# A spectral layer: TensorE's eight turns over the filters written out, and VectorE's matrix mixing put behind the third part of a unit

## The chip, the cores and the metric

The kernel runs on one core of one Trainium2 chip. The metric is the device time of one execution in microseconds (us). The kernel before takes 7840.03 us, the median of three runs from 7836.26 to 7846.94.

## The reference, cut to what matters

The program is a network of four layers over an image of 4 x 48 x 48 positions with 128 channels. The change touches only the last stage of layer 3, the spectral layer. It convolves every channel of the normalized stream with 16 causal filters, once as they are and once with the sign of every second position turned, and mixes the channels of each result with a 128x128 matrix:

```python
def _stu_conv(phi, u, n):
    sgn3 = where(arange(sl) % 2 == 0, 1.0, -1.0)[None, :, None]
    Vf, Uf_p, Uf_m = rfft(phi), rfft(u), rfft(u * sgn3)
    U_plus  = irfft(Vf[None, :, :, None] * Uf_p[:, :, None, :])[:, :sl]
    U_minus = irfft(Vf[None, :, :, None] * Uf_m[:, :, None, :])[:, :sl] * sgn
    return U_plus, U_minus

out = einsum('btkd,k,kde->bte', U_plus, sigma ** 0.25, Mpp) \
    + einsum('btkd,k,kde->bte', U_minus, sigma ** 0.25, Mpm)
# ... plus three shifted copies of u, each times a matrix; done for the whole
# sequence and its first half, quarter and eighth, each with its own matrices,
# and added with four weights; then t = t + result
```

Since the sum and the difference of U_plus and U_minus are convolutions with the even and the odd taps alone, the kernel mixes the two matrices of a filter into their sum (z = 0) and their difference (z = 1), and it adds the matrices of the four sequence lengths up, weighted, so that each stretch of the sequence meets one matrix.

## The kernel before, in words

`layer3_spectral` loops over the four images with `nc.Fori(0, NB)` (line 2301). Each image has a short block that orders and turns the input (L2303 to L2361), and then the block that matters here (from L2363). There each of the 16 filters gives four **units** (u % 4 = 0 to 3): the even or odd taps with the even or odd positions. One turn over a **pair** of filters is eight units, and an image has eight pairs. `r` (0 or 1) is the filter's place in the pair and the buffer it uses.

The work of a unit, engine by engine:

- TensorE (L2396 on) forms the convolution in three parts, by the sum-and-difference trick that saves products. `shared` (L2432), `shared_pairs` (L2442), `first` (L2422), `second` (L2432, L2442) and `third` (L2422, L2432) fill the PSUM banks OWN, PAIR and LOW for unit u + 1 while unit u is being mixed. The last `pairs` of unit u (L2442) comes at the head of its turn, and `mix` (L2457) multiplies each of the three finished parts with the filter's mixing matrices, in fp16 high and low pieces. Every unit is 108 matmuls.
- ScalarE (L2594 on) copies PSUM to SBUF (`keep`, `pair_1`), and writes the fp16 high piece of each finished part (`high`, L2607) and of the mixing matrices (L2611). It takes its instructions strictly in that order: `high` of the third part stands between `keep` of the next unit and the copy `pair_1` (L2619) of the next unit.
- VectorE (L2518 on) adds and subtracts to finish the parts: L2557 and L2558 the first, L2561 to L2564 the second, L2567 to L2579 the third. Between these it mixes the matrices of the next filter, `mix_step`: step 0 is two 128x512 operations (sum and difference, L2526 and L2527), each of steps 1 to 4 two 128x128 ones (L2537, L2539).
- GpSimd (L2636 on) subtracts the high piece from the value and so makes the low piece (`low`, L2641, 128x384; of the matrices L2645, 128x512).
- SyncE's DMA queue loads the next filter's taps (F, FS) and matrices (mab).

All engines run this as code with waits on semaphores, in the order in which the code stands. On TensorE and ScalarE the turns over pairs are a `Fori` loop of seven turns with the eighth written out behind it (the eighth prepares no next unit); on VectorE, GpSimd and the DMA queue they are a `Fori` loop of eight. In a filter the mixing steps stand so: unit 0 has steps 0 and 1, unit 1 steps 2 and 3, unit 2 step 4, unit 3 none; of each two the first stands between L2572 and L2576, that is inside the third part, and the second behind L2579.

What TensorE waits for in a unit: the copy `pair_1` before `pairs`; the high and low pieces before each `mix`; the combination L2569, which frees bank PAIR, before `shared_pairs`; L2572 before `first`.

Of the kernel before, what the change touches and what calls it, by code (L numbers as in the profile page):

```python
# [2074 lines left out]
KF, KU = 16, 3  # L2075
# [8 lines left out]
def layer3_spectral(nc, w, f_scr, f_sum, out):  # L2084
# [12 lines left out]
    with ExitStack() as ctx:  # L2097
# [203 lines left out]
        with nc.Fori(0, NB) as b:  # L2301
# [61 lines left out]
            with nc.Block() as block:  # L2363
# [31 lines left out]
                def _(pe):  # L2395
# [66 lines left out]
                    def shared(u):  # L2462
                        own(u, OWN, 2, 2 * HB + u % 2 * LB, True).then_inc(s_cv, 1)
# [24 lines left out]
                    def filters_pair(i, last):  # L2488
                        unit = (b * KF + i * 2) * NU
                        for u in range(2 * NU):  # L2490
                            r = u // NU
                            done = (unit + u) * 12 + 24
                            copied = (unit + u) * 4
                            v = (u + 1) % (2 * NU)
                            more = not (last and v == 0)
                            pe.wait_ge(s_ea, copied + 4)
                            pairs(u, FS[:, :, :, :, 1], 0, True).then_inc(s_cv, 1)
                            mix(i, u, 0)
                            if more:
                                if v % NU == 0:  # L2500
                                    pe.wait_ge(s_fl[v // NU], (b * (KF // 2) + i + (1 if v else 2)) * 64)
                                pe.wait_ge(s_ed, done + 3)
                                shared(v)
                                pe.wait_ge(s_ed, done + 7)
                                shared_pairs(v)
                            mix(i, u, 1)
                            if more:
                                pe.wait_ge(s_ed, done + 9)
                                first(v)
                                second(v, copied + 4)  # L2510
                                third(v, copied + 4)
                            mix(i, u, 2)

                    with pe.Fori(0, KF // 2 - 1) as i:
                        filters_pair(i, False)
                    filters_pair(KF // 2 - 1, True)

                @block.vector  # L2518
                def _(dve):
                    def mix_step(kk, i, r, step, total):  # L2520

                        if step == 0:
                            dve.wait_ge(s_ml[r], use(i, r) * 32 + 32)

                            dve.wait_ge(s_kd[r], b * (KF // 2) + i)
                            dve.tensor_tensor(Wm[:, r, 0], mab[:, r, 0], mab[:, r, 1], ALU.add).then_inc(s_ad[r], 1)  # L2526
                            dve.tensor_tensor(Wm[:, r, 1], mab[:, r, 0], mab[:, r, 1], ALU.subtract).then_inc(s_ad[r], 1)  # L2527
                            return
                        m = step - 1
                        if m == 0:  # L2530
                            dve.wait_ge(s_ad[r], use(i, r) * 2 + 2)
                        else:
                            dve.wait_ge(s_mm, total + 2 * m)
                        for z in range(2):
                            own, weight = Wm[:, r, z, m], mweight[:, ds(kk, 1), z, m:m + 1]
                            if m == 0:
                                ins = dve.tensor_scalar(own, own, weight, None, ALU.mult)  # L2537
                            else:
                                ins = dve.scalar_tensor_tensor(own, own, weight, Wm[:, r, z, m - 1], ALU.mult, ALU.add)  # L2539
                            ins.then_inc(s_mm, 1)  # L2540
                        if m == 3:
                            dve.wait_ge(s_mm, total + 8)
                            dve.sem_inc(s_wm[r], 1)


                    base = b * (KF + 1) * 8
                    for step in range(5):
                        mix_step(0, 0, 0, step, base)
                    with dve.Fori(0, KF // 2) as i:
                        unit = (b * KF + i * 2) * NU  # L2550
                        for u in range(2 * NU):
                            r, step = u // NU, u % NU * 2
                            at = (unit + u) * 12 + 24
                            second, third = Uc[:, 0, :], Uc[:, 1, :]
                            low_ps, edge_s = ps[:, LOW:LOW + BANK], low_s[:, RC:]
                            dve.wait_ge(s_ea, (unit + u) * 4 + 3)
                            dve.tensor_tensor(low_s[:, P:2 * P], low_s[:, P:2 * P], edge_s, ALU.add).then_inc(s_ed, 1)  # L2557
                            dve.tensor_tensor(low_s[:, 2 * P:RC], low_s[:, 2 * P:RC], edge_s, ALU.subtract).then_inc(s_ed, 1)  # L2558
                            dve.wait_ge(s_cv, (unit + u) * 6 + 4)
                            dve.wait_ge(s_ea, (unit + u) * 4 + 4)  # L2560
                            dve.tensor_tensor(second, ps[:, OWN:OWN + RC], pair_1, ALU.add).then_inc(s_ed, 1)  # L2561
                            dve.wait_ge(s_ed, at + 3)
                            dve.tensor_tensor(second[:, P:], second[:, P:], pair_1[:, 0:2 * P], ALU.subtract).then_inc(s_ed, 1)
                            dve.tensor_tensor(second[:, 0:P], second[:, 0:P], pair_1[:, 2 * P:], ALU.subtract).then_inc(s_ed, 1)  # L2564
                            dve.wait_ge(s_cv, (unit + u) * 6 + 5)
                            dve.wait_ge(s_ul, (unit + u) * 3 + 3)
                            dve.tensor_tensor(third, low_ps[:, 0:RC], own_s[:, u % 2, :], ALU.subtract).then_inc(s_ed, 1)  # L2567
                            dve.wait_ge(s_cv, (unit + u) * 6 + 6)
                            dve.tensor_tensor(pair_2, ps[:, PAIR:PAIR + RC], pair_s[:, u % 2, :], ALU.subtract).then_inc(s_ed, 1)  # L2569
                            dve.wait_ge(s_ed, at + 6)  # L2570
                            dve.tensor_tensor(third[:, P:2 * P], third[:, P:2 * P], low_ps[:, RC:], ALU.add).then_inc(s_ed, 1)
                            dve.tensor_tensor(third[:, 2 * P:], third[:, 2 * P:], low_ps[:, RC:], ALU.subtract).then_inc(s_ed, 1)  # L2572
                            if step < 5:
                                mix_step(i * 2 + r + 1, i + r, 1 - r, step, base + (i * 2 + r + 1) * 8)
                            dve.wait_ge(s_ed, at + 9)
                            dve.tensor_tensor(third, third, pair_2, ALU.add).then_inc(s_ed, 1)  # L2576
                            dve.wait_ge(s_ed, at + 10)
                            dve.tensor_tensor(third[:, P:], third[:, P:], pair_2[:, 0:2 * P], ALU.subtract).then_inc(s_ed, 1)
                            dve.tensor_tensor(third[:, 0:P], third[:, 0:P], pair_2[:, 2 * P:], ALU.subtract).then_inc(s_ed, 1)  # L2579
                            if step + 1 < 5:  # L2580
                                mix_step(i * 2 + r + 1, i + r, 1 - r, step + 1, base + (i * 2 + r + 1) * 8)
                    for r in range(2):
                        dve.wait_ge(s_kd[r], (b + 1) * (KF // 2))  # L2583
                    for p in range(2):
                        for lo, hi, src in ((0, RC, ps[:, 2 * p * BANK:2 * p * BANK + RC]),
                                            (RC, 2 * RC, ps[:, (2 * p + 1) * BANK:(2 * p + 1) * BANK + RC]),
                                            (2 * RC, 2 * RC + 2 * P, ps[:, 2 * p * BANK:2 * (p + 1) * BANK].rearrange("p (o x) -> p o x", o=2)[:, :, RC:]),
                                            (2 * RC + 2 * P, HL, ps[:, 4 * BANK + p * P:4 * BANK + (p + 1) * P])):
                            xs = xres[:, ds(b * L + 2 * lo, 2 * (hi - lo))].rearrange("p (a q) -> p q a", q=2)[:, p, :]
                            if hi - lo == 2 * P:  # L2590
                                xs = xs.rearrange("p (o x) -> p o x", o=2)
                            dve.scalar_tensor_tensor(xs, src, shrink[:, 0:1], xs, ALU.mult, ALU.add).then_inc(s_res, 1)  # L2592
# [211 lines left out]
```

## Time and profile before

| | before |
|---|---|
| median of 3 runs | 7840.03 us |
| profiled execution | 7841.85 us, span 7839.8 us |
| mean granted TensorE clock | 0.959 |
| busy share PE, PEld, DVE, ACT, POOL | 90%, 77%, 80%, 58%, 59% |
| the spectral filters (from the first to the last mixing matmul, L2457) | 5819.2 to 7827.8 us |
| TensorE idle, "issue", before L2442 and before L2422 | 75.0 us, 38.0 us |
| instructions loaded, queue 8 and queue 14 | 9.34 MB and 2.23 MB |

PE is TensorE's matmuls, PEld its weight loads, DVE is VectorE, ACT is ScalarE and POOL is GpSimd. The shares are means over stages with different limits, so they say little about one stage. "Issue" is idle time for which the profile shows nothing that the engine waited for.

### The profile page before, as it was taken

Reading aid. Unit: us, or ns where it says so; the run is one execution under the profiler, and the core shown is the slowest. Engines: PE = TensorE matmul, PEld = TensorE weight load, DVE = VectorE, ACT = ScalarE, POOL = GpSimd, SP = SyncE. Lnnn points to the kernel's source line nnn. Section 1 sums busy time; section 2 is a strip of 40 time slices with the busy share of each in tenths; the row PEclk is TensorE's granted clock in tenths of the full one; section 3 lists DMA queues with packets and bytes.
Section 4 is the critical chain, followed back from the end, with each engine's and each line's share of the span. In section 5 each row is a group of like instructions: output and inputs, shape, how many; then the busy total and the mean of one; then the engine's idle time right before and its main releaser. Section 6 shows DMA issues by size and latency. Waiting matters only on the chain. (4 is left out here: it accounts for less than half of the span.)

```text
span 7839.8 us, 179804 instructions
## 1 busy us (share of the span) xinstructions
PE 7046.8 (90%) x64572; PEld 6018.8 (77%) x64572; DVE 6238.0 (80%) x9093; ACT 4510.7 (58%) x9442; POOL 4630.3 (59%) x5010
## 2 busy tenths in 40 slices
PE   8999989999899998999857999798978989899898
PEld 6888768887688876888747888456658878888888
DVE  7999879998799987999846776455667878788787
ACT  5888658886588866887612333244444544444444
POOL 5888658886588865888647765121124444444444
PEclk9999999999999999999979999899989999999999
DMA  2333223332233322333267775000024333334343
GB/s 65 91 93 90 80 61 90 93 91 79 61 90 93 92 79 62 90 93 92 77 201 228 223 198 166 6 14 22 11 73 123 111 120 111 119 111 129 101 129 99
DMA packets 595211, 775.58 MB, mean 99 GB/s; under 512 B 52215, under 2 KB 528408, under 8 KB 592193
## 3 DMA queue, kind: packets, MB, share of 16 engines
q1 hardware_dynamic: 542529, 594.11, 25.6%
q0 software_dynamic: 51840, 169.91, 7.6%
q8 instruction: 570, 9.34, 0.5%
q14 instruction: 272, 2.23, 0.1%
HBM read 730.16 MB, written 33.66 MB: 97 GB/s over the span
## 5 line engine op out<-in xcount | busy, mean ns | idle before, releaser
L647 POOL TENSOR_TENSOR l_arena<-l_arena 128x768 f32<-128x768 f32 x1536 | 2589.2, 1686 | 451.5 <-DVE l_arena L579 445.1
L579 DVE TENSOR_TENSOR_SCAN l_arena<-l_arena,psum 128x772 f32<-128x772 f32 x1536 | 2662.4, 1749 | 176.8 <-PE psum L406 74.5
L500 ACT ACTIVATE l_arena<-l_arena,l_A 128x384 f32<-128x384 f32 x3072 | 1643.0, 603 | 38.2 <-DVE l_arena L579 32.8
L408 PE MATMUL psum<-l_arena 128*128 128x128 f32 x11520 | 1499.8, 280 | 46.4 <-DVE l_arena L579 42.6
L408 PEld LDWEIGHTS psum<-l_arena 128*128 128x128 f32 x11520 | 1367.9, 193 | 169.9 <-issue 146.1
L419 PE MATMUL psum<-l_ident,l_arena 128*128 128x128 f32 x9216 | 1257.6, 273 | 50.5 <-ACT l_yT L506 41.6
L419 PEld LDWEIGHTS psum<-l_ident,l_arena 128*128 128x128 f32 x9216 | 1055.1, 141 | 60.2 <-POOL l_arena L647 60.2
L2641 POOL TENSOR_TENSOR st_U<-st_Uc,st_U 128x384 f16<-128x384 f32 x512 | 469.3, 917 | 970.7 <-ACT st_U L2607 970.7
L1211 POOL DMA_INDIRECT l_G<-neighbours,l_idx x648 | 622.0, 960 | 391.2 <-issue 188.9
L490 ACT ACTIVATE l_arena<-l_arena,l_BT 128x256 f32<-128x256 f32 x1728 | 746.7, 496 | 7.5
L2457 PE MATMUL psum<-st_U,st_W 128*128 128x128 f16 (+3 forms) x6144 | 532.0, 229 | 32.5 <-POOL st_U L2641 23.1
L2432 PE MATMUL psum<-st_FS,st_xt 128*128 128x128 f16 x6912 | 530.0, 222 | 0.4 <-DMA st_FS<-filter_sums 0.4
L2607 ACT ACTIVATE st_U<-st_Uc 128x384 f16<-128x384 f32 x512 | 266.2, 520 | 446.6 <-DVE st_Uc L2564 390.1
L556 DVE TENSOR_TENSOR l_arena<-psum,l_BT 128x384 f32<-128x384 f32 x960 | 509.0, 531 | 0.0
L406 PEld LDWEIGHTS psum<-l_ident,l_arena 128*128 128x128 f32 x3456 | 380.5, 140 | 143.8 <-issue 141.3
L406 PE MATMUL psum<-l_ident,l_arena 128*128 128x128 f32 x3456 | 487.0, 277 | 2.8 <-DVE l_arena L579 2.8
L2422 PE MATMUL psum<-st_F,st_xt 128*128 128x128 f16 x4608 | 436.1, 220 | 38.0 <-issue 38.0
L1054 DVE TENSOR_TENSOR l_G<-l_G,psum 128x1536 f32<-128x1536 f32 (+1 forms) x144 | 366.3, 2547 | 125.2 <-DMA l_G<-neighbours,l_idx 124.8
L2457 PEld LDWEIGHTS psum<-st_U,st_W 128*128 128x128 f16 x6144 | 413.2, 99 | 50.2 <-POOL st_U L2641 31.8
L2432 PEld LDWEIGHTS psum<-st_FS,st_xt 128*128 128x128 f16 x6912 | 431.6, 99 | 0.7 <-DMA st_FS<-filter_sums 0.6
L2442 PE MATMUL psum<-st_FS,st_xt 128*128 128x128 f16 x4608 | 351.1, 221 | 75.0 <-issue 75.0
L1259 PE MATMUL psum<-l_ident,l_G 128*128 128x128 f32 x2592 | 315.2, 281 | 71.1 <-DVE l_G L1054 43.0
(456 smaller groups left out, 11910.2 us busy)
## 6 DMA issues: line engine op xcount, KB each, us to landing
l_arena<-c_rows SPq DMA_DIRECT2D x1536, 192.0 KB, 3.0
st_FS<-filter_sums SPq DMA_DIRECT2D x128, 1155.0 KB, 9.6
st_F<-filter_parts SPq DMA_DIRECT2D x128, 320.5 KB, 6.7
neighbours<-l_xt SPq DMA_DIRECT2D x256, 72.0 KB
st_mab<-in_st_mp SPq DMA_DIRECT2D x68, 256.0 KB, 9.2
st_mab<-in_st_mm SPq DMA_DIRECT2D x68, 256.0 KB, 6.8
l_G<-neighbours,l_idx POOLq DMA_INDIRECT x648, 3.7
l_arena<-in_x SPq DMA_DIRECT2D x4, 1152.0 KB, 5.2
```

What stands on the lines that cost most here:

```text
L406: mm = pe.transpose(ps[:, o:o + P], xT[:, rank[s] % 2, t, h * P:(h + 1) * P], ident[:])
L408: mm = pe.matmul(ps[:, o:o + P], dtuT[:, g % 2, t, h * P:(h + 1) * P], diagB[:, rank[s] % 3, t, :], start=True, stop=True)
L419: mm = pe.matmul(y_ps[:, t, h * P:(h + 1) * P], hC[:, s % NHC, h, t * P:(t + 1) * P], ident[:], start=(n == 0 and h == 0 and t % 2 == 0), ...
L490: ins = act.activation(xT[:, i % 2, t, :], dtuT[:, g % 2, t, :], ACT.Copy, scale=BT[:, g % 2, t, n:n + 1])
L500: act.activation(decay[:, s % NDC, half(h)], dtv[:, g % 2, h, :], ACT.Exp, scale=A[:, g // NRC, h, n:n + 1]).then_inc(s_exp, 1)
L556: dve.tensor_tensor(diagB[:, i % 3], ident_ps.unsqueeze(1).broadcast_to([P, LB, P]), BT[:, g % 2, :, n:n + 1].broadcast_to([P, LB, P]), AL ...
L579: dve.tensor_tensor_scan(hbuf[:, n, run], decay[:, s % NDC, run], x2_ps[s % 2][:, run], 0.0, ALU.mult, ALU.add).then_inc(s_scan, 1)
L647: pool.tensor_tensor(hC[:, s % NHC], halves(hbuf[:, s % NS, :]), Cs[:, s % NCS, :].unsqueeze(1).broadcast_to([P, 2, RC]), ALU.mult).then_i ...
L1211: pool.indirect_dma_start(out=G[:, g, 4 * k:4 * k + 4, :].rearrange("p q c -> p (q c)"), out_offset=None, in_=tables[b], in_offset=bass.In ...
L2432: mm = pe.matmul(ps[:, at + i * P:at + (i + 1) * P], xt[:, xpart, x0 + LB - 1 - i, :], FS[:, r, fpart, z, three, shift + i * P:shift + (i ...
L2457: mm = pe.matmul(ps[:, o:o + hi - lo], W16[:, r, wpart, z, m, :], U16[:, c, upart, lo - c * RC:hi - c * RC], start=False, stop=False, skip ...
L2641: pool.tensor_tensor(U16[:, c, 1, :], src, U16[:, c, 0, :], ALU.subtract).then_inc(s_ul, 1)
```

## The change

TensorE's loop over seven pairs and the written-out eighth become a Python loop: all eight turns are written out as straight code, inside the loop over images, which stays. The other engines keep their loops. On VectorE the first mixing step of a unit moves from inside the third part to behind its last operation, so that two steps (in units 0 and 1) or one (unit 2) stand behind it in a row.

```diff
-                    with pe.Fori(0, KF // 2 - 1) as i:
-                        filters_pair(i, False)
-                    filters_pair(KF // 2 - 1, True)
+                    for i in range(KF // 2):
+                        filters_pair(i, i == KF // 2 - 1)
...
                             dve.tensor_tensor(third[:, P:2 * P], third[:, P:2 * P], low_ps[:, RC:], ALU.add).then_inc(s_ed, 1)
                             dve.tensor_tensor(third[:, 2 * P:], third[:, 2 * P:], low_ps[:, RC:], ALU.subtract).then_inc(s_ed, 1)
-                            if step < 5:
-                                mix_step(i * 2 + r + 1, i + r, 1 - r, step, base + (i * 2 + r + 1) * 8)
                             dve.wait_ge(s_ed, at + 9)
                             dve.tensor_tensor(third, third, pair_2, ALU.add).then_inc(s_ed, 1)
                             dve.wait_ge(s_ed, at + 10)
                             dve.tensor_tensor(third[:, P:], third[:, P:], pair_2[:, 0:2 * P], ALU.subtract).then_inc(s_ed, 1)
                             dve.tensor_tensor(third[:, 0:P], third[:, 0:P], pair_2[:, 2 * P:], ALU.subtract).then_inc(s_ed, 1)
+                            if step < 5:
+                                mix_step(i * 2 + r + 1, i + r, 1 - r, step, base + (i * 2 + r + 1) * 8)
                             if step + 1 < 5:
                                 mix_step(i * 2 + r + 1, i + r, 1 - r, step + 1, base + (i * 2 + r + 1) * 8)
```

TensorE at the end of one pair and the start of the next, before (L2457 is the mixing of unit 7's third part, L2442 `pairs`):

```order
2706 L2457 MATMUL psum<-st_U,st_W 128x128 x6
2707 L2455 REGISTER_ALU
2708 L2457 MATMUL psum<-st_U,st_W 128x128 x3
2709 L2514 REGISTER_ALU
2710 L2514 COMPARE_AND_BRANCH
2711 L2496 ISA
2712 L2442 MATMUL psum<-st_FS,st_xt 128x128 x9
```

and the same place in the code after:

```order
2703 L2457 MATMUL psum<-st_U,st_W 128x128 x6
2704 L2455 REGISTER_ALU
2705 L2457 MATMUL psum<-st_U,st_W 128x128 x3
2706 L2496 ISA
2707 L2442 MATMUL psum<-st_FS,st_xt 128x128 x9
```

The loop's counter and its branch are gone; the matmuls are the same. Before, this branch led back to the top of a body of 864 matmuls, each with a weight load of its own.

VectorE in unit 0 of a filter, before (lines as in the kernel before):

```order
2398 L2572 TENSOR_TENSOR st_Uc<-st_Uc,psum 128x128
2399 L2523 ISA
2400 L2526 TENSOR_TENSOR st_Wm<-st_mab 128x512
2401 L2527 TENSOR_TENSOR st_Wm<-st_mab 128x512
2402 L2575 REGISTER_ALU
2403 L2576 TENSOR_TENSOR st_Uc<-st_Uc,st_xr 128x384
2404 L2577 REGISTER_ALU
2405 L2578 TENSOR_TENSOR st_Uc<-st_Uc,st_xr 128x256
2406 L2579 TENSOR_TENSOR st_Uc<-st_Uc,st_xr 128x128
2407 L2531 ISA
2408 L2537 ISA
2409 L2537 TENSOR_SCALAR st_Wm<-st_Wm,st_mweight 128x128
```

and after (every line number above 2514 is one lower, those of the three operations that finish the third part three lower):

```order
2398 L2571 TENSOR_TENSOR st_Uc<-st_Uc,psum 128x128
2399 L2572 REGISTER_ALU
2400 L2573 TENSOR_TENSOR st_Uc<-st_Uc,st_xr 128x384
2401 L2574 REGISTER_ALU
2402 L2575 TENSOR_TENSOR st_Uc<-st_Uc,st_xr 128x256
2403 L2576 TENSOR_TENSOR st_Uc<-st_Uc,st_xr 128x128
2404 L2522 ISA
2405 L2525 TENSOR_TENSOR st_Wm<-st_mab 128x512
2406 L2526 TENSOR_TENSOR st_Wm<-st_mab 128x512
2407 L2530 ISA
2408 L2536 ISA
2409 L2536 TENSOR_SCALAR st_Wm<-st_Wm,st_mweight 128x128
```

The three additions that finish the third part have moved ahead of the two 128x512 operations; the wait of step 1 on these two (L2531, after L2530) now stands right behind them.

## Rows read from the trace of the kernel before

**Rows 1.** Waits of TensorE, whole span: us in total, times, longest.
```profile
PE psum L2442 <- issue: 75.0, 24, 3.5
PE psum L2422 <- issue: 38.0, 23, 4.0
```

**Rows 2.** Timeline of TensorE behind one branch back: start us, us, what, idle before.
```profile
6574.10 1.14 PE L2442 MATMUL psum<-st_FS,st_xt 128*128 128x128 f16 x9 [2.91 <-issue]
...
6579.89 0.29 PE L2422 MATMUL psum<-st_F,st_xt 128*128 128x128 f16 x1 [0.60 <-issue]
```

**Rows 3.** Windows of TensorE: us, busy (x), granted clock, DMA share, GB/s.
```profile
6762.50:6771.30 8.80, 8.69 (x152) 1.00 0.03 9
6574.00:6582.00 8.00, 7.30 (x80) 0.62 1.08 307
```

**Rows 4.** Timeline of TensorE: the same matmuls (unit 4) of first and seventh pair, each image.
```profile
5853.79 0.34 PE L2457 MATMUL psum<-st_U,st_W 128*128 128x128 f16 x3 [0.50 <-POOL st_U L2641]
...
6213.11 0.34 PE L2457 MATMUL psum<-st_U,st_W 128*128 128x128 f16 x3 [0.51 <-POOL st_U L2641]
...
6367.07 0.34 PE L2457 MATMUL psum<-st_U,st_W 128*128 128x128 f16 x3 [0.51 <-POOL st_U L2641]
...
6729.24 0.34 PE L2457 MATMUL psum<-st_U,st_W 128*128 128x128 f16 x3 [0.50 <-POOL st_U L2641]
...
6882.68 0.34 PE L2457 MATMUL psum<-st_U,st_W 128*128 128x128 f16 x3 [0.50 <-POOL st_U L2641]
...
7240.89 0.34 PE L2457 MATMUL psum<-st_U,st_W 128*128 128x128 f16 x3 [0.50 <-POOL st_U L2641]
...
7394.49 0.34 PE L2457 MATMUL psum<-st_U,st_W 128*128 128x128 f16 x3 [0.50 <-POOL st_U L2641]
...
7753.64 0.34 PE L2457 MATMUL psum<-st_U,st_W 128*128 128x128 f16 x3 [0.50 <-POOL st_U L2641]
```

**Rows 5.** Timeline of VectorE, eighth pair: L2561 of units 0, 1 and 4.
```profile
6748.27 0.56 DVE L2561 TENSOR_TENSOR st_Uc<-psum,st_xr 128x384 f32<-128x384 f32 x1 [0.50 <-ACT st_xr L2619]
...
6755.89 0.56 DVE L2561 TENSOR_TENSOR st_Uc<-psum,st_xr 128x384 f32<-128x384 f32 x1 [0.17 <-ACT st_xr L2619]
...
6775.57 0.56 DVE L2561 TENSOR_TENSOR st_Uc<-psum,st_xr 128x384 f32<-128x384 f32 x1 [0.50 <-ACT st_xr L2619]
```

**Rows 6.** DMA queues, 6390 to 6790 us: packets, MB, share of 16 engines.
```profile
q1 hardware_dynamic: 50903, 45.79, 38.4%
q8 instruction: 58, 0.95, 1.0%
```

**Rows 7.** Timeline of ScalarE behind its own branch back, looped pair.
```profile
6508.57 0.49 ACT L2619 ACTIVATE st_xr<-psum 128x384 f32<-128x384 f32 x1
```

**Rows 8.** Timeline of a unit 0, eighth pair (the last PE row is in unit 1).
```profile
6751.18 0.27 DVE L2572 TENSOR_TENSOR st_Uc<-st_Uc,psum 128x128 f32<-128x128 f32 x1
...
6752.15 1.64 DVE L2527 TENSOR_TENSOR st_Wm<-st_mab 128x512 f32<-128x512 f32 x1
...
6754.84 0.48 DVE L2537 TENSOR_SCALAR st_Wm<-st_Wm,st_mweight 128x128 f32<-128x128 f32 x2
...
6756.48 1.16 DVE L2563 TENSOR_TENSOR st_Uc<-st_Uc,st_xr 128x256 f32<-128x256 f32 x1
...
6756.54 0.34 PE L2457 MATMUL psum<-st_U,st_W 128*128 128x128 f16 x3 [0.50 <-POOL st_U L2641]
...
6758.83 0.68 PE L2442 MATMUL psum<-st_F,st_xt 128*128 128x128 f16 x9 [0.43 <-DVE st_xr L2569]
```

**Rows 9.** Timeline of a unit 3, the one ahead of it.
```profile
6744.64 0.27 DVE L2572 TENSOR_TENSOR st_Uc<-st_Uc,psum 128x128 f32<-128x128 f32 x1
...
6745.10 1.47 POOL L2645 TENSOR_TENSOR st_W<-st_Wm,st_W 128x512 f16<-128x512 f32 x1
...
6746.78 0.28 DVE L2579 TENSOR_TENSOR st_Uc<-st_Uc,st_xr 128x128 f32<-128x128 f32 x1
...
6747.74 0.91 POOL L2641 TENSOR_TENSOR st_U<-st_Uc,st_U 128x384 f16<-128x384 f32 x1 [1.17 <-ACT st_U L2607]
```

**Rows 10.** Timeline at an image's start: VectorE's mixing steps in a row, GpSimd idle.
```profile
6314.81 0.69 DVE L2526 TENSOR_TENSOR st_Wm<-st_mab 128x512 f32<-128x512 f32 x1 [3.83 <-DMA st_mab<-in_st_mm]
...
6316.14 0.48 DVE L2537 TENSOR_SCALAR st_Wm<-st_Wm,st_mweight 128x128 f32<-128x128 f32 x2
```

## Prediction, made before the changed kernel ran

> **What bounds the kernel now.** I read the waits of TensorE over the whole span first. Two entries stand out that wait for no engine: 75.0 us of "issue" before L2442 in 24 places and 38.0 us before L2422 in 23 [rows 1]. L2442 is `pairs`, the first matmul of a pair of filters, and 24 is 4 images times the 6 branches back of a loop of seven turns. So the branch itself stops TensorE. The timeline behind one branch shows both stops: 2.91 us of idle before the first matmuls, then nine matmuls of 128 columns in 1.14 us, and some 6 us later another stop, here 0.60 us, elsewhere up to 4.0 [rows 2, 1]. In the 8 us behind that branch the granted clock is 0.62, a mean over stretches at 1.2 GHz and at 2.4 GHz, against 1.00 in a stretch of straight code, where TensorE is busy 8.69 of 8.80 us [rows 3]. So a branch costs its idle time and then some matmuls at the lower clock.
>
> Then I read what a unit is bound by where no branch disturbs it, the eighth pair. VectorE's L2561 starts every 6.56 us in units 1 to 3 (6755.89 to 6775.57, three units), but unit 0 takes 7.62 us [rows 5]. TensorE is all but full in the 6.56 us. The extra 1.06 us of unit 0 is VectorE's: its step 0 stands in front of the third part.
>
> **Part 1, the loop written out.** I take the time between the same matmuls of the first and the seventh pair of an image, six pairs and six branches apart: 359.32, 362.17, 358.21 and 359.15 us [rows 4], sum 1438.85. Straight code takes 27.30 us per filter (6748.27 to 6775.57, rows 5), so 54.60 per pair and 24 x 54.60 = 1310.4 for the same work. The difference is **128.4 us**, 5.35 per branch; 113.0 of it are the two idle entries [rows 1] and 15 the lower clock.
>
> Nothing is added for it, provided that straight code is fed in time. For this the eighth pair is the test, since TensorE falls into it without a branch: no stop there, with the same 864 matmuls less those that prepare a next unit. Nor do filter loads matter. They come twice per pair, once behind the branch (DMA share 1.08, rows 3) and once in the middle of the pair; in the middle TensorE runs on at the straight pace. TensorE's code is loaded anew in every turn already: 58 instruction packets in 400 us (0.95 MB), all on queue 8 and none on queue 14 [rows 6]. So the volume of code stays as it is, and the loops of VectorE, ScalarE and GpSimd load nothing.
>
> What is late next, with TensorE's stop gone, would be the branches of the other engines, till now hidden under it. VectorE and GpSimd branch back ahead of the eighth pair too, and L2561 starts on time there (6748.27, rows 5, with its usual 0.50 us wait). ScalarE doesn't branch at that place, but in a looped pair its first instruction behind the branch, L2619, runs before TensorE's stop, at 6508.57, and with no idle time worth a mark before it [rows 7]. I cost these at nothing; 0.1 us at each of 24 places would be 2 us. The second filter of a pair is loaded from a pair's start and wanted 20 us later, in the eighth pair as everywhere.
>
> Queue 8 goes on loading in every turn of the same body, about 8.7 packets per pair of 60 us [rows 6]. The Trainium skill (Runtime: NRT & Kernel Launch, section "Instruction fetch mechanics") gives TensorE room for 2048 instructions; 864 matmuls and 864 weight loads with their waits could fit, and by that rule the body would stay loaded and the stops have another cause. The trace differs, and the trace decides.
>
> **Part 2, the mixing steps.** Unit 2 (step 4 moved) and unit 3 (no step) don't change: VectorE is idle before L2557 and before L2561 there, and the sum of its work is the same. In unit 1, steps 2 and 3 in a row end about 0.1 us later than now, which the 0.50 us wait before L2561 [rows 5] takes up. Unit 0 decides, 64 times.
>
> Before, from the start of L2572 (6751.18) it is 3.66 us to L2537 (6754.84), 4.71 to the next L2561 (6755.89), and 7.65 to TensorE's restart at 6758.83, which waits for L2569 [rows 8, 5]. TensorE's other wait, 0.50 us for the low piece of the third part at 6756.54, goes with the change, since that part is done earlier. But it isn't on the path that ends last: TensorE would only arrive earlier at the wait for L2569.
>
> After, from L2572:
> - L2579 starts at 2.14, as in unit 3, where nothing stands between and GpSimd's 128x512 operation is under way as it is here (6746.78 - 6744.64, rows 9).
> - Step 0 starts 0.20 behind, at 2.34. From it to step 1 it takes 1.33 with GpSimd idle (6316.14 - 6314.81, rows 10), so 3.67.
> - GpSimd's low piece of the third part comes in at 3.10 (6747.74 - 6744.64, rows 9), while the second half of step 0 runs. An operation of that size takes 0.69 alone [rows 10] and 1.64 where GpSimd is first [rows 8]; for one that was first itself I take a slowing of 0.16, an estimate near the lower end of that 0.95. Step 1 now waits for the instruction right ahead and sets registers, about 0.10. So L2537 at 3.93.
> - From L2537 to L2561 1.05 now, of which 0.17 is a wait for ScalarE that has gone [rows 5, 8]: 0.88. GpSimd's operation, pushed back by L2527, ends near 4.55 and holds up L2557 for 0.05. L2561 at **4.86 instead of 4.71**.
> - From L2561 to TensorE's restart 2.94 now; L2563, 1.16 us for 128x256, waits there for GpSimd [rows 8]. The same meeting stays, since both sides move together.
>
> So unit 0 becomes **0.15 us longer**, and 64 x 0.15 = 10 us are lost. The ends: if L2563 gets in ahead of GpSimd and GpSimd isn't pushed back by L2527, the unit is up to 0.3 us shorter (-19 us); if step 1's operations must wait for GpSimd too, each of the two stands until 4.55 and everything is 0.4 later (+0.55, +35 us). I take the middle term because each of its rows has an exact model in the trace.
>
> The trace shows that a VectorE addition of two SBUF operands and a GpSimd operation exclude each other: 1.47 us for GpSimd at 6745.10 beside a VectorE addition [rows 9]. The Trainium skill (SBUF — State Buffer, section "SBUF: two separate sides") says the same, whoever starts first holds the shared ports for a whole instruction, and adds operations in a two-port mode. In VectorE: DVE Perf Modes (section "The perf-mode tier table") it gives fp32 `tensor_scalar` that mode; by this L2537 would be held too, the +35 us case. The trace speaks against it: two L2537 take 0.48 us, no less than additions of that size (0.28 each, started 0.20 apart).
>
> **The sum.** 7841.85 (profiled execution) - 128.4 + 10 = 7723.4. That execution is 1.8 us above the median 7840.03, so **7721 us**, 119 us or 1.5% faster.
>
> **The rivals.**
> - VectorE loses more: L2537 held by GpSimd, 0.55 us x 64 = 35 us; 7840 - 128 + 35 = 7747. For it: VectorE's queue is full in unit 0. Against: the durations of L2537. Chance 0.15.
> - VectorE gains: the waits of TensorE in unit 0 go and L2563 isn't held; -19 us or more, 7712 - 19 = 7693; with all of unit 0's 1.06 us gone, 64 x 1.06 = 68, it would be 7644, but 1.8 us of mixing plus the rest of VectorE's unit don't fit into 6.56. Chance 0.17.
> - The code isn't fed in time everywhere: stops stay at one pair boundary in three, 24 x 5.35 / 3 = 43 us; 7764. Against: none in the eighth pairs. Chance 0.03.
> - The stops aren't the branch's but come with each new pair, whatever the code; then only part 2 counts, 7850. For it: they all stand at the same place. Against: the eighth pair begins without one. Chance 0.02.
> - Slower than before: the next piece of straight code is asked for while a filter load fills the DMA rings. With two loads per pair there are 64; a stop of 2.9 us at each (rows 2) is 186 us, 7840 + 10 - 128 + 186 = 7908. It decides from 118 / 64 = 1.85 us per load on. For it: the second stop behind a branch does fall into a load (share 1.08, rows 3). Against: the load in the middle of each pair and in the eighth pair stops nothing. Chance 0.02.
> - The forecast: 0.61.
>
> **How the numbers follow.** Range: 7688 to 7752, from the gain to the loss on VectorE with a few us beside; the last three rivals and the far end of the second (together about 0.1) stay outside. A measurement can tell from no change about 0.2%, 16 us. Faster than that: forecast and first three rivals, 0.96 together; no change (the fourth) 0.02; slower 0.02.
>
> **What would show it.** Right: no "issue" entry at L2442 and L2422 in the waits; the pairs of an image 54.8 to 55 us apart from the first to the last; unit 0 at 7.6 to 7.8 us and L2561's wait for ScalarE gone there; TensorE's wait for the low piece gone and the wait for L2569 longer in its place; queue 8 as many MB as before. Wrong: stops of 1 to 4 us at other places in the straight code; pitches of units 1 to 3 other than 6.56; unit 0 below 7.4 (the low piece of the third part was on the path after all) or above 8.0 (L2537 of 0.5 us or more).

## The result and the profile after

The changed kernel takes **7729.02 us** (median of four runs, 7727.4 to 7734.91); the kernel before took 7841.93 us in the same rounds. The ratio is 0.9858 with a 95% interval of 0.9841 to 0.9875, so it is 1.4% faster. The forecast was 7721 us.

The profiled execution has a span of 7728.1 us, 111.7 us less than before. TensorE's waits in the spectral stage (5800 to 7728 us) now begin so; columns as in [rows 1]:

```profile
PE psum L2457 <- POOL st_U L2640: 44.0, 72, 0.6
PE psum L2350 <- DVE st_xr L2310: 33.4, 3, 11.1
PE psum L2457 <- ACT st_U L2606: 30.0, 72, 2.1
PE psum L2442 <- DVE st_xr L2568: 17.9, 72, 0.6
```

No entry "issue" is left at L2442 or L2422: the 113.0 us of [rows 1] are gone. Filter loads do not stop the straight code. The window with a load under way (DMA share 0.89) has the same granted clock of 1.00 as the one with little of it; what it lacks in busy time are the waits of a unit 0, seen below. Columns as in [rows 3]:

```profile
6370.00:6378.00 8.00, 7.89 (x137) 1.00 0.27 91
6421.00:6429.00 8.00, 6.82 (x113) 1.00 0.89 269
```

The pace of the units, from VectorE's timeline in the middle of the second image (L2560 is what L2561 was; compare [rows 5]):

```profile
6413.11 0.56 DVE L2560 TENSOR_TENSOR st_Uc<-psum,st_xr 128x384 f32<-128x384 f32 x1 [0.54 <-ACT st_xr L2618]
6421.01 0.54 DVE L2560 TENSOR_TENSOR st_Uc<-psum,st_xr 128x384 f32<-128x384 f32 x1
6427.60 0.56 DVE L2560 TENSOR_TENSOR st_Uc<-psum,st_xr 128x384 f32<-128x384 f32 x1 [0.35 <-ACT st_xr L2618]
...
6440.67 0.56 DVE L2560 TENSOR_TENSOR st_Uc<-psum,st_xr 128x384 f32<-128x384 f32 x1 [0.49 <-ACT st_xr L2618]
```

Unit 0 takes 7.90 us (7.62 before), the other three 19.66 (19.68 before), a filter 27.56 instead of 27.30. So the account closes: -128.4 us for the branches, 64 x 0.26 = +16.6 us for the filters, together -111.8 against -111.7 measured. That it closes to 0.1 us is luck: the spans of one kernel differ by more, and over all its filters the trace has a mean of 27.58 us, 0.24 and not 0.26 above the kernel with the loop written out alone (27.34).

Inside that unit 0, the timeline of VectorE, GpSimd and TensorE; it answers to [rows 8]:

```profile
6416.01 0.27 DVE L2571 TENSOR_TENSOR st_Uc<-st_Uc,psum 128x128 f32<-128x128 f32 x1
...
6418.15 0.28 DVE L2576 TENSOR_TENSOR st_Uc<-st_Uc,st_xr 128x128 f32<-128x128 f32 x1
6418.36 0.68 DVE L2525 TENSOR_TENSOR st_Wm<-st_mab 128x512 f32<-128x512 f32 x1
...
6418.96 0.68 DVE L2526 TENSOR_TENSOR st_Wm<-st_mab 128x512 f32<-128x512 f32 x1
6419.10 1.30 POOL L2640 TENSOR_TENSOR st_U<-st_Uc,st_U 128x384 f16<-128x384 f32 x1 [1.16 <-ACT st_U L2606]
...
6419.81 0.88 DVE L2536 TENSOR_SCALAR st_Wm<-st_Wm,st_mweight 128x128 f32<-128x128 f32 x2 [0.17 <-DVE st_Wm L2526]
...
6421.59 0.42 DVE L2562 TENSOR_TENSOR st_Uc<-st_Uc,st_xr 128x256 f32<-128x256 f32 x1
...
6421.70 0.51 PE L2457 MATMUL psum<-st_U,st_W 128*128 128x144 f16 x6 [0.33 <-ACT st_U L2606]
...
6421.93 1.00 DVE L2563 TENSOR_TENSOR st_Uc<-st_Uc,st_xr 128x128 f32<-128x128 f32 x1
...
6422.84 0.34 PE L2457 MATMUL psum<-st_U,st_W 128*128 128x144 f16 x3 [0.63 <-POOL st_U L2640]
...
6423.92 0.68 PE L2442 MATMUL psum<-st_F,st_xt 128*128 128x128 f16 x9 [0.23 <-DVE st_xr L2568]
```

The third part is done early (L2576 starts 2.14 us behind L2571), but GpSimd's low piece of it, 0.91 us in other units, now takes 1.30: it sets out while L2526 holds the ports. It in turn holds up L2536, 0.88 us for two operations that take 0.48 alone: the first takes 0.69 us, the second 0.28. TensorE's wait has moved from the third part's mixing into the next unit's first mixing, 0.33 and 0.63 us.

### The profile page after: what moved, and what is told of

Its sections match the earlier page's. It is cut to its first block and busy times, and to the rows that moved or that the text cites. A ratio compares the mean times of both kernels' runs of the same rounds, so it can differ in the third digit from the quotient of the medians.

```text
span 7728.1 us, 179680 instructions
## 1 busy us (share of the span) xinstructions
PE 7006.9 (91%) x64572; PEld 5977.8 (77%) x64572; DVE 6274.2 (81%) x9093; ACT 4517.9 (58%) x9442; POOL 4672.5 (60%) x5010
## 5 line engine op out<-in xcount | busy, mean ns | idle before, releaser
L2640 POOL TENSOR_TENSOR st_U<-st_Uc,st_U 128x384 f16<-128x384 f32 x512 | 496.9, 970 | 743.9 <-ACT st_U L2606 743.9
L2457 PE MATMUL psum<-st_U,st_W 128*128 128x128 f16 (+3 forms) x6144 | 522.6, 226 | 74.0 <-POOL st_U L2640 44.0
L2432 PE MATMUL psum<-st_FS,st_xt 128*128 128x128 f16 x6912 | 518.2, 219 | 0.8 <-DMA st_FS<-filter_sums 0.8
L2457 PEld LDWEIGHTS psum<-st_U,st_W 128*128 128x128 f16 x6144 | 401.7, 97 | 98.9 <-POOL st_U L2640 56.2
L2422 PE MATMUL psum<-st_F,st_xt 128*128 128x128 f16 x4608 | 427.2, 219 | 0.0
L1259 PEld LDWEIGHTS psum<-l_ident,l_G 128*128 128x128 f32 x2592 | 300.0, 145 | 92.9 <-DVE l_G L1054 48.7
```

Of the source, the lines that this page charges most:

```text
L1259: mm = pe.matmul(bank(i % 2, P * a, P * (a + 1)), G[:, g, 4 * k + q, :], ident[:], start=(q == 0), stop=(q == 3), is_transpose=True, skip_ ...
L2432: mm = pe.matmul(ps[:, at + i * P:at + (i + 1) * P], xt[:, xpart, x0 + LB - 1 - i, :], FS[:, r, fpart, z, three, shift + i * P:shift + (i ...
L2457: mm = pe.matmul(ps[:, o:o + hi - lo], W16[:, r, wpart, z, m, :], U16[:, c, upart, lo - c * RC:hi - c * RC], start=False, stop=False, skip ...
L2640: pool.tensor_tensor(U16[:, c, 1, :], src, U16[:, c, 0, :], ALU.subtract).then_inc(s_ul, 1)
```

## The experiments

Differences of a span below are against the profiled execution of the kernel before, 7839.8 us. Spans of one and the same kernel differ by some us from run to run (7833.7 to 7852.9 in 15 runs of the kernel before), so differences of a few us are read from the medians and their intervals. Kernels of one round share their runs of the kernel before.

**The loop written out alone.** VectorE as before the change; the edit is the first part of the diff.

```diff
-                    with pe.Fori(0, KF // 2 - 1) as i:
-                        filters_pair(i, False)
-                    filters_pair(KF // 2 - 1, True)
+                    for i in range(KF // 2):
+                        filters_pair(i, i == KF // 2 - 1)
```

> TensorE's turns written out, VectorE's mixing steps where they were. Theory (the gain is the 24 branch stops of 5.35 us, and the moved mixing steps lose 0.26 us in each of 64 units 0): about 128 us faster than before, 16 us faster than the changed kernel, so near 7712; every filter 27.30 us apart. Rival (the moved steps are free or gain, and the written-out loop alone is worth only 112 us): no faster than the changed kernel, 7728 or more, filters 27.56 us apart or more.

Measured: 7713.99 us, ratio 0.9834 (0.982 to 0.9847), span 7710.0, 129.8 us less. Unit 0 is back at 7.62 us and the filter at 27.31:

```profile
6516.59 0.56 DVE L2560 TENSOR_TENSOR st_Uc<-psum,st_xr 128x384 f32<-128x384 f32 x1 [0.53 <-ACT st_xr L2618]
6524.21 0.56 DVE L2560 TENSOR_TENSOR st_Uc<-psum,st_xr 128x384 f32<-128x384 f32 x1 [0.18 <-ACT st_xr L2618]
...
6543.90 0.56 DVE L2560 TENSOR_TENSOR st_Uc<-psum,st_xr 128x384 f32<-128x384 f32 x1 [0.50 <-ACT st_xr L2618]
```

So the first part alone is worth more than the whole change, as the theory said. TensorE's waits for the pieces and for L2568 say the same:

```profile
PE psum L2457 <- POOL st_U L2640: 35.9, 72, 0.5
PE psum L2442 <- DVE st_xr L2568: 30.8, 72, 0.6
PE psum L2457 <- ACT st_U L2606: 9.4, 8, 2.1
```

They sum to 76.1 us here and to 91.9 (44.0 + 17.9 + 30.0) in the changed kernel, 15.8 us more, about 0.25 per filter.

**The moved mixing alone.** The second part of the diff, TensorE's loop kept.

```diff
-                            if step < 5:
-                                mix_step(...)          # ahead of the third part's last three operations
+                            if step < 5:
+                                mix_step(...)          # behind them
```

> VectorE's mixing steps moved, TensorE's loop of seven turns kept. Theory: slower than before by 0.26 us for each unit 0 that no branch stop covers, 40 of 64, so 10 us, at most 17 us: 7850 to 7857. Rival (moving the steps gains by itself, since TensorE no longer waits in unit 0): 10 us or more faster than before.

Measured: 7855.01 us, ratio 1.0014 (1.0005 to 1.0023), span 7852.7, 12.9 us more. By the medians of its own round it is 8.9 us more, with an interval of 4 to 18. So the second part is a small loss by itself, but whether it costs the 10 us of 40 uncovered units 0 or the 17 of 64 the runs can't tell. The two parts add up within the noise: 0.9834 x 1.0014 = 0.9848, against 0.9858 (0.9841 to 0.9875) for both.

**Two pairs in a turn.** A third of the branches, over a body twice as long.

```diff
-                    with pe.Fori(0, KF // 2 - 1) as i:
-                        filters_pair(i, False)
+                    with pe.Fori(0, KF // 4 - 1) as j:
+                        filters_pair(j * 2, False)
+                        filters_pair(j * 2 + 1, False)
+                    filters_pair(KF // 2 - 2, False)
                     filters_pair(KF // 2 - 1, True)
```

> TensorE's loop takes two pairs in a turn, three turns, and the last two pairs are written out: 2 branches back per image, 8 in all, over a body twice as long; mixing steps as before the change. Theory (a fixed price per branch): 16 of 24 stops go, 16 x 5.35 = 86 us, so near 7756, and 8 places of issue before L2442. Rival (the stop grows with the length of the body that is branched over): more than 8 x 5.35 = 43 us stay, up to 86 us, 7756 to 7798, with stops above 4 us.

Measured: 7762.77 us, ratio 0.9894 (0.9879 to 0.9909), span 7761.4. The waits of TensorE, whole span:

```profile
PE psum L2442 <- issue: 24.8, 8, 3.4
PE psum L2422 <- issue: 15.2, 8, 2.9
```

3.1 us at each first stop, as with the body of one pair (75.0 / 24 = 3.1), and 1.9 at the second, where that body has 38.0 / 23 = 1.7. The price is per branch. Against the written-out loop the 8 branches cost 51.4 us by the spans and 48.8 by the medians, 6.1 to 6.4 each; the intervals of the two ratios allow 4 to 8, so this isn't told from 5.35. The longest stop is no longer than before.

**A shorter body.** The loop of seven turns stays; the convolutions of the spectral filters keep one of their three fp16 products.

```diff
-                    PARTS = ((0, 0), (0, 1), (1, 0))
+                    PARTS = ((0, 0),)
```

> The kernel before with one of three fp16 products in each convolution of the spectral filters (the low pieces of inputs and taps are left out there; the mixing keeps its three): TensorE's loop body has 416 matmuls instead of 864, in all about half the instructions. Theory (a branch back always drops what was loaded and asks for it anew): queue 8 still loads in every turn, about half as many packets, and 24 stops of about 3 us stay before the first matmul of a pair. Rival (a body that fits into TensorE's instruction memory is kept): next to no packets on queue 8 while the loop runs, and no stop at the branch.

Measured: 7665.77 us. Here my theory fell. The waits of TensorE, whole span, and the queues from 6400 to 6700 us (columns as in [rows 6]):

```profile
PE psum L2442 <- issue: 5.4, 24, 0.3
```

```profile
q1 hardware_dynamic: 42773, 38.49, 43.2%
q8 instruction: 3, 0.05, 0.1%
```

Three packets in 300 us, where the kernel before has 45 in the same stretch (58 in the 400 us of [rows 6]), and 0.22 us at each branch where it was 3.1: the branches are all there, but the body is kept. So the branch is dear only where its target must be loaded again.

**Two products of three, and two in one helper.** Bodies between these two lengths. I count lengths in blocks, a block being what one packet brings (0.95 MB in 58 packets of [rows 6], 16 KB). Straight code needs 43 packets for six pairs, so the full body has 7.2 blocks. By the matmuls and weight loads left out I estimate 3.7 for one product, 5.4 for two, and 6.6 for two in `own` alone.

```diff
-                    PARTS = ((0, 0), (0, 1), (1, 0))
+                    PARTS = ((0, 0), (0, 1))
```

> The kernel before with two of three fp16 products in each convolution (the low pieces of the inputs are left out): a loop body of about 5.4 blocks of 256 instructions, against 7.2 now and about 3.7 with one product. Theory (the body must fit into TensorE's instruction memory together with what is loaded ahead behind its end, about 2 blocks): kept, next to no packets on queue 8 while the loop runs, no stop over 0.3 us at the branch. Rival (room for less than 5 blocks): packets in every turn and 24 stops of about 3 us.

Measured: 7658.82 us, kept:

```profile
PE psum L2442 <- issue: 5.5, 24, 0.3
```

The other one cuts the products in `own` alone:

```diff
-                            for m, (xpart, fpart) in enumerate(PARTS):
+                            for m, (xpart, fpart) in enumerate(PARTS[:2]):     # in own()
```

> The kernel before with two of three fp16 products in the 27 matmuls of a unit that helper own issues (the low pieces of the inputs are left out there): a loop body of about 6.6 blocks of 256 instructions, between 5.4 (two products everywhere, kept) and 7.2 (not kept). Theory (room for 8 blocks, of which about 2 are taken by what is loaded ahead behind the loop's end): not kept, 24 stops of about 3 us before L2442 and about 8 packets on queue 8 per turn. Rival (the whole room is the loop's): kept, no packets, no stop over 0.3 us.

Measured: 7782.56 us, not kept:

```profile
PE psum L2442 <- issue: 71.1, 19, 4.1
PE psum L2422 <- issue: 22.3, 17, 2.9
```

The stops are there, 3.7 us at 19 places. At the other five of the 24 branches there is none: the weight load there waits 0.28 to 0.29 us, and only the entry of the weight loads has all 24 places:

```profile
PEld psum L2442 <- issue: 75.8, 24, 4.2
```

The packets go with it. In the second image queue 8 brings 7 to 9 packets in a turn that begins with a stop (7 from 6436.7 to 6491.8 us), and 2 in each of the two turns that begin without one (6491.8 to 6549.8, 6605.2 to 6662.9). So this body is loaded again at 19 branches and kept at five. The body of 5.4 blocks was kept at all 24, that of 7.2 at none. The border lies near 6.6 blocks or below; what sets it, and why these five branches got through, is not shown.

The lengths change TensorE's work too, so the times of these three don't price a branch; their waits and packets do.

**Step 0 stays, the small steps move.** TensorE written out.

```diff
-                            if step < 5:
+                            if step == 0:
                                 mix_step(...)          # ahead of the third part's last three operations
...
+                            if 0 < step < 5:
+                                mix_step(...)          # behind them, then step + 1
```

> TensorE written out; step 0 of the mixing stays inside the third part in unit 0, steps 2 and 4 (units 1 and 2) stand behind it as in the changed kernel. Theory (unit 0 alone decides): a filter takes 27.30 us as with the loop written out alone, near 7712. Rival (the two small steps in a row in unit 1 delay the next unit): filters of 27.4 to 27.6 us, 7718 to 7730.

Measured: 7711.97 us, ratio 0.983 (0.9815 to 0.9845), span 7712.7. No difference from the loop alone (7710.0): the moves in units 1 and 2 are free, and unit 0 decides.

**Step 0 cut in two.** A try to empty unit 0, TensorE written out.

```diff
+                            for step in ((0,), (0.5, 1, 2), (3, 4), ())[u % NU]:     # 0: sum, 0.5: difference
+                                mix_step(...)          # all behind the third part
```

> TensorE written out; step 0 cut into its two 128x512 operations. Behind the third part: unit 0 the sum, unit 1 the difference and steps 1 and 2, unit 2 steps 3 and 4, unit 3 nothing. Theory (unit 0 is long because 1.3 us of step 0 and 0.5 us of step 1 stand in the one unit, while units 1 and 2 have 0.5 us to spare before L2561): filters of 26.4 to 26.8 us instead of 27.30, so 32 to 58 us below 7712, near 7667. Rival (VectorE is as full in unit 1 as in unit 0, and what unit 0 gives unit 1 takes): 27.3 us or more, 7712 or more.

Measured: 7783.24 us, ratio 0.9922 (0.9908 to 0.9935), 71 us more than the 7712 of the loop alone, where I had hoped for 32 to 58 us less. The other cut has `((0,), (0.5, 1), (2, 3, 4), ())`:

> As the other cut of step 0, with unit 0 the sum, unit 1 the difference and step 1, unit 2 steps 2, 3 and 4. Theory: unit 1 has 0.6 us less and unit 2 0.6 us more than there; since unit 2 has no other operation of GpSimd's near its end, filters of 26.3 to 26.8 us, within 10 us of the other cut. Rival (three steps in unit 2 delay the mixing matrices that ScalarE takes in unit 3): 27.0 us or more, 7690 or more.

Measured: 7759.89 us, ratio 0.9892 (0.9877 to 0.9908). Both theories fell. In the first, unit 0 is shorter as planned, 6.98 us, but unit 1 takes 7.59 and unit 2 takes 7.21. In the second, unit 1 takes 6.59, but unit 2, with steps 2, 3 and 4, takes 7.83. The timeline of the first cut, at unit 1's end and at unit 2's, shows why (here L2558 and L2559 are the first part of the next unit):

```profile
6438.31 1.27 DVE L2540 SCALAR_TENSOR_TENSOR st_Wm<-st_Wm,st_mweight 128x128 f32<-128x128 f32 x2
6438.37 1.07 POOL L2640 TENSOR_TENSOR st_U<-st_Uc,st_U 128x384 f16<-128x384 f32 x1 [2.57 <-ACT st_U L2606]
...
6445.98 1.07 POOL L2640 TENSOR_TENSOR st_U<-st_Uc,st_U 128x384 f16<-128x384 f32 x1 [2.60 <-ACT st_U L2606]
6445.98 0.29 DVE L2558 TENSOR_TENSOR st_low_s<-st_low_s 128x128 f32<-128x128 f32 x1 [0.24 <-DVE st_Wm L2540]
...
6446.19 1.00 DVE L2559 TENSOR_TENSOR st_low_s<-st_low_s 128x128 f32<-128x128 f32 x1
```

The two operations of a step (L2540) take 0.61 where nothing holds them and 1.27 here; L2559 takes 1.00 for 0.28. GpSimd's low piece of the third part starts at a time that ScalarE sets, and whatever VectorE still has to do on SBUF then waits some 0.7 us. The time to spare in units 1 and 2 isn't the 0.50 us of wait before L2561 that I had counted, but the time up to that start.

**Step 1 out of unit 0.** The changed kernel, with its steps as `((0,), (1, 2), (3, 4), ())`, all behind the third part.

> The changed kernel with step 1 of the mixing taken out of unit 0: behind the third part stand step 0 in unit 0, steps 1 and 2 in unit 1, steps 3 and 4 in unit 2. Theory (step 1 costs unit 0 the most of what it loses, 0.88 us for its two operations since GpSimd's low piece of the third part holds them up, and the next operation would be held up in their place for 0.3 us less in all): filters 0.3 us shorter than the changed kernel's 27.56, so 27.26 and about 7710. Rival (the length of unit 0 is set by the 128x512 operations alone): filters of 27.5 us, 7725 to 7730.

Measured: 7751.45 us, ratio 0.9882 (0.9865 to 0.9898). Unit 0 fell from 7.90 to 7.57 us (L2560 at 6447.79 and 6455.36), the 0.3 forecast; L2556 is now held in step 1's place, 1.00 us for 0.28. But unit 2 rose from 6.54 to 7.14:

```profile
6440.05 1.07 POOL L2638 TENSOR_TENSOR st_U<-st_Uc,st_U 128x384 f16<-128x384 f32 x1 [2.60 <-ACT st_U L2604]
6440.05 0.29 DVE L2556 TENSOR_TENSOR st_low_s<-st_low_s 128x128 f32<-128x128 f32 x1 [0.24 <-DVE st_Wm L2538]
...
6440.26 1.01 DVE L2557 TENSOR_TENSOR st_low_s<-st_low_s 128x128 f32<-128x128 f32 x1
```

Steps 3 and 4 in a row, with the wait on step 4 behind them (0.24 us before L2556), end so late that L2557 starts 0.21 us behind GpSimd's operation. It takes 1.01 us for 0.28, and the unit is 0.60 longer. Step 4 alone behind the third part, and steps 2 and 3 in a row, which have no such wait, are free in the changed kernel.

## Why the prediction was right, point by point

- **What bounds the kernel: right.** The stops were the branch's.
- **Part 1, 128.4 us: right.** The loop written out alone gave 129.8 in the span and 132.1 in the medians (interval 120 to 141). That nothing stops the straight code during filter loads, and that the loops of the other engines cost nothing, showed as forecast; units 1 to 3 keep their pace from the first pair to the last.
- **Why a branch stops.** I set the Trainium skill's room for 2048 instructions against the trace and took it for refuted, since queue 8 ran on. That conclusion was too broad: bodies of 3.7 and 5.4 blocks are kept. The skill's rule (Runtime: NRT & Kernel Launch, section "Instruction fetch mechanics"), that a branch out of the loaded window forces a load, agrees with the packets and stops measured here. The two pages that it gives as that window don't: bodies of 3.7 and 5.4 blocks were kept. The room of 8 blocks that the page gives TensorE is nearer, but a loop gets less of it: a body of about 6.6 was kept at 5 branches of 24.
- **Part 2, 10 us: right in sign, too small.** It cost 16.6 us, 0.26 per filter instead of 0.15. By the terms: L2579 at 2.14 (measured 2.14), step 0 at 2.34 (2.35), GpSimd at 3.10 (3.09), step 1 at 3.93 (3.80; L2526 wasn't slowed, 0.68), from step 1 to L2560 0.93 (**1.20**), from there to TensorE's restart 2.94 (2.91). The last term is right in size, but the meeting in it moved: the 128x256 operation now passes ahead of GpSimd in 0.42 us (1.16 before), and the 128x128 one behind it waits, 1.00 us for 0.28. So the rival of a gain had that step right too, and it gave nothing. The mis-sized term is step 1: "two L2537 take 0.48 us, no less than additions of that size" was no evidence that the operation escapes GpSimd. Its first is held until GpSimd ends, 0.69 us for 0.28. The rival that I gave 0.15 had the mechanism right, and the Trainium skill (VectorE: DVE Perf Modes, section "The perf-mode tier table") as well. It had the price too high, 35 us: GpSimd's operation ended at 4.39 and not at 4.55, and only the first of the two was held, not each. The trace shows that L2536 is held; the two-port mode itself can't be seen in it.
- **Where TensorE waits: wrong in place.** I expected a longer wait for L2569. It is shorter, 0.23 us at L2568 instead of 0.43, and the wait became the next unit's first mixing instead, 0.33 us for the high and 0.63 for the low piece.
- **Queue 8: wrong.** 523 packets instead of 570. The 47 less are about two per branch taken, and the kernel with 8 branches has 538, about two per branch as well. That these are code which was loaded behind the loop's end and not run is my reading. "As many MB as before" overlooked it.

The median came out 8 us above the forecast, 7 of which are the 0.11 us per filter; that the other terms left only 1 us is within the noise.

The best kernels here are the loop written out alone, 7714 us, ratio 0.9834, and the one in which step 0 stays, 7712 us, ratio 0.983; the runs don't tell them apart. The whole change has 0.9858. The intervals of these ratios overlap a little; that the moved step 0 loses is read from the filters' length, 27.34 us against 27.58 in the mean.

## What to carry to other kernels

A loop on TensorE cost next to nothing here where its body stayed loaded and some 5 to 6 us per turn where it didn't; look at the instruction queue in a stretch of turns, then shorten the body, or write the turns out. An instruction of VectorE that is moved to "free" time must be set against the starts of GpSimd's operations, not against VectorE's idle time: one that started 0.21 us behind such a start cost 0.60 us, and an early end cost nothing. Judge parts of a change one by one: here the second took back an eighth of what the first gave.

## What the runs showed of the hardware that I had not expected

- A branch back on TensorE to code that is still loaded takes 0.22 us (24 of 24), to code that isn't 3.1 us, and a second stop of 1.7 us follows some 6 us later. Near the border one and the same loop does both: 19 branches with a stop of 3.7 us, five without.
- A `tensor_scalar` of 128x128 fp32 in SBUF with a scalar per partition is held by a GpSimd operation like an addition of two SBUF tensors is, though alone it takes the same 0.28 us as such an addition.
- GpSimd and VectorE alternate: with a queue of SBUF operations on VectorE, GpSimd gets the ports behind the one that was running (1.30 us for 0.91), and VectorE's next waits for GpSimd's end.
